# The last expert's rows by one-hot products, and the first token-MLP products taken pass by pass

## The reference, cut to what matters

```python
x = x + attention(conditioned(x))
x = x + routed_ffn(expert_ffn(x))        # 2nd: routed_ffn is the part below
x = x + mingru(token_mlp(x))             # 3rd: token_mlp, two picked experts of width 1024 and a shared one
x = x + ffn(adapted(x))

def routed_ffn(h):                       # 8 experts, top 2, room for 640 tokens each
    ...
    exp_batches = zeros(8, 640, 256).at[flat_e, pos_safe].set(x[tok], mode='drop')
    h = gelu(inp) * gate                 # inp, gate = split(exp_batches @ W1), width 512
    exp_out = h @ W2                     # [8, 640, 256]
    gathered = exp_out[flat_e, min(pos_safe, 639)]
    contrib = where(keep, gates_f, 0)[:, None] * gathered
    return segment_sum(contrib, tok)     # each token: two gated rows of exp_out
```

## Time and profile before

| | |
|---|---|
| time, median of 3 runs | 999.74 us (998.01 to 1001.44) |
| profiled execution, own time | 1008.6 us |
| span of the profile | 1007.4 us |
| PE busy | 953.5 us, 95% of the span |
| DVE / ACT / POOL busy | 497.4 / 436.1 / 272.2 us |
| DMA | 67.48 MB moved, mean 67 GB/s |
| DMA queue of SP (q1) / of POOL (q0) | 11.2% / 9.3% of 16 engines |

### The profile page before, as it was taken

How to read it: one execution, slowest core, us unless ns; L and a number is a source line. 1 busy time by engine, 2 the same in 40 slices (tenths; PEclk the granted TensorE clock), 3 DMA queues, 4 the chain that set the end, 5 groups by cost and what they waited for, 6 DMA issues and landing times.

```text
span 1007.4 us, 13258 instructions
## 1 busy us (share of the span) xinstructions
PE 953.5 (95%) x4952; PEld 783.0 (78%) x4952; DVE 497.4 (49%) x947; ACT 436.1 (43%) x820; POOL 272.2 (27%) x243
## 2 busy tenths in 40 slices
PE   5989999999899999999699999999999999998998
PEld 2667767787589999987587788888888888876786
DVE  5645453566444554544467433333333333688544
ACT  2555564523154444544234334244343342326675
POOL 1333221402256555536452014023041140100000
PEclk9999999999999999999999999999999999999999
DMA  7130001102325444441521300302003003000011
GB/s 261 43 106 21 22 1 64 73 22 84 122 47 125 133 114 133 115 152 35 190 57 39 126 1 1 126 0 110 16 1 126 1 0 126 1 1 1 1 42 43
DMA packets 21648, 67.48 MB, mean 67 GB/s; under 512 B 4497, under 2 KB 11921, under 8 KB 19281
## 3 DMA queue, kind: packets, MB, share of 16 engines
q1 hardware_dynamic: 16592, 39.88, 11.2%
q0 software_dynamic: 4704, 26.49, 9.3%
q10 hardware_dynamic: 288, 0.26, 0.1%
HBM read 55.09 MB, written 9.44 MB: 64 GB/s over the span
## 4 chain that ended last, share of the span: by engine, by line
PE 72%; DVE 12%; ACT 6%; issue 4%; DMA 3%; another core or an unknown queue 1%; SPq 1%; DVEq 0%; ACTq 0%; POOLq 0%
PE banks L934 15%; PE banks L936 14%; PE banks L935 14%; PE banks L1132 4%; PE banks L1133 4%; PE banks L1131 4%; PE banks L1014 3%; PE banks L998 2%; PE banks L1181 1%; PE banks L1180 1%; PE banks L1167 1%; PE banks L1168 1%; PE banks L950 1%; PE banks L1005 1%; DMA expert_output<-y_rows 1%
## 5 line engine op out<-in xcount | busy, mean ns | idle before, releaser
L934 PE MATMUL banks<-input_hi,mlp_hi 128*128 128x512 f32 (+1 forms) x396 | 156.1, 394 | 3.9 <-DVE input_lo L1741 2.4
L936 PE MATMUL banks<-input_hi,mlp_lo 128*128 128x512 f32 (+1 forms) x396 | 155.3, 392 | 0.0
L935 PE MATMUL banks<-input_lo,mlp_hi 128*128 128x512 f32 (+1 forms) x396 | 154.8, 391 | 0.0
L1937 POOL TENSOR_TENSOR mlp_lo<-weight_stage,mlp_hi 128x768 fp32r<-128x768 f32 x40 | 73.6, 1841 | 241.8 <-ACT mlp_hi L1369 241.8
L1384 ACT CAST hidden_hi<-hidden 128x512 fp32r<-128x512 f32 x96 | 59.6, 621 | 176.4 <-DVE hidden L1751 108.0
L1757 DVE TENSOR_TENSOR hidden_lo<-hidden,hidden_hi 128x512 fp32r<-128x512 f32 x96 | 66.5, 693 | 71.3 <-ACT hidden_hi L1384 71.3
L1751 DVE SCALAR_TENSOR_TENSOR hidden<-banks,L_expert_weight,gelu 128x512 f32<-128x512 f32 x64 | 48.0, 751 | 97.6 <-PE banks L936 97.4
L1907 POOL TENSOR_TENSOR ffn_w_lo<-weight_stage,ffn_w_hi 128x512 fp32r<-128x512 f32 x48 | 62.0, 1294 | 109.2 <-ACT ffn_w_hi L1331 109.2
L934 PEld LDWEIGHTS banks<-input_hi,mlp_hi 128*128 128x128 f32 x396 | 75.2, 190 | 20.2 <-issue 4.3
L936 PEld LDWEIGHTS banks<-input_hi,mlp_lo 128*128 128x128 f32 x396 | 75.3, 190 | 16.4
L935 PEld LDWEIGHTS banks<-input_lo,mlp_hi 128*128 128x128 f32 x396 | 75.5, 191 | 16.0
(11 more groups left out here) (298 smaller groups left out, 2099.2 us busy)
## 6 DMA issues: line engine op xcount, KB each, us to landing
weight_stage<-in_packF SPq DMA_DIRECT2D x8, 1536.0 KB, 6.9
weight_stage<-in_shared SPq DMA_DIRECT2D x2, 3072.0 KB, 10.9
expert_output<-y_rows SPq DMA_DIRECT2D x40, 128.0 KB
weight_stage<-in_cond_w SPq DMA_DIRECT2D x4, 512.0 KB, 6.4
...
```

The costliest lines, as they stand in the source:

```text
L934: pe.matmul(o, wh, dh, start=(i == 0), stop=False)
L935: pe.matmul(o, wh, dl, start=False, stop=False)
L936: last = pe.matmul(o, wl, dh, start=False, stop=(i == len(terms) - 1))
L1937: pool.tensor_tensor(wDl[s][:, qs], stage[:, qs], f(wDh[s][:, qs]), ALU.subtract).then_inc(done)
```

## The change

1. *Chunk 0 without the last expert's rows in DRAM.* For chunk 0 the contribution of expert 7 no longer goes through the table. For each of its five slot tiles DVE makes a one-hot matrix `hot` (is slot s of token t, 128x512), beside expert 6's down products. After each `w2` of expert 7, ACT makes the gated rounded row tile (`hot_hi`) and DVE the difference (`hot_lo`); after the last `w2` PE multiplies them by `hot` into banks 0 and 1 (`hot`, 20 products of 512 columns), DVE adds the two banks to `xT` (`hot_add`), ACT and DVE make the halves (`hot_in`, `hot_in_lo`).
2. *Chunk 0's other seven experts are combined beside expert 7* (`beside_last_expert`): `fetch`, `comb`, `yt` and `add` of tiles 0 to 3 are woven into it; the fetch waits for the stores of experts 0 to 6. For chunk 0 the row numbers and the gates of expert 7 are set to zero.
3. *The gate of each slot of expert 7* comes by a table in DRAM: SP writes 2048 gates, one element a descriptor, after the routing; POOL reads them by five indirect DMAs and numbers 512 columns (`counting`), at the start of expert 2. Both gate and token rows are shifted by one, so that row 0 is an unused slot's.
4. *The first MLP weights earlier and in halves.* `ld_mlp` becomes two loads of 1.5 MB, for all phases. Half 0 goes out once expert 6's weights are split, half 1 once expert 7's are. Pieces 0 to 4 are split beside expert 6's down products, pieces 5 to 7 in the first three steps of expert 7.
5. *First products pass by pass.* The early halves are gone; the first two units wait for `hot_in` of each block and use `inL` last (`first_products`).
6. *Fillers.* `slots` 8 to 16, `first rows` 27 to 13; the 30 and 7 ahead of the first tiles go, 4 come ahead of the first MLP product.
7. The combining of chunks 1 to 3 starts one unit later.

```diff
-EARLY = 3
+HOT = 0
...
-SPIN = {"first scores": 12, "logits": 5, "slots": 8, "first rows": 27, "first tile": 30, "next tile": 7}
+SPIN = {"first scores": 12, "logits": 5, "slots": 16, "first rows": 13, "first hidden": 4}
...
-        if e + 1 == G:
-            pool.append(("ld_mlp", 0))
+        if e + 2 >= G:
+            pool.append(("ld_mlp", 0, e + 2 - G))
...
+            if e == G - 1:
+                act.append(("hot_hi", j))
+                dve.append(("hot_lo", j))
             dve.append(("yrow", e, j))
+            if e == G - 2:
+                dve.append(("onehot", j))
+                mlp_piece(j)
...
+    def mlp_piece(q):
+        act.append(("wm_hi", 0, q))
+        pool.append(("wm_lo", 0, q))
+    def beside_last_expert():
+        for tt in range(3):
+            pool.append(("fetch", tt))
+        for q in range(ST, PIECES):
+            mlp_piece(q)
+            if q == ST:
+                pool.append(("fetch", 3))
+            yield
+        yield
+        for tt in range(2):
+            dve.append(("comb", tt))
+            yield
+        for tt in range(3):
+            product("turn3", "yt", tt)
+            if tt == 0:
+                dve.append(("comb", 2))
+            dve.append(("add", tt))
+            yield
+        dve.append(("comb", 3))
+        yield
+        yield
+        product("turn3", "yt", 3)
+        dve.append(("add", 3))
...
-            run(weave(expert, split_mlp(0)))
...
+            run(weave(expert, beside_last_expert()))
...
+    banks["hot", 0] = (HOT, HOT + 1)
+    assert ring_at["work"] % 4 == HOT
+    ring_at["work"] += KD
+    for j in range(ST):
+        pe.append(("hot", j))
+    for k in range(KD):
+        dve.append(("hot_add", k))
+        act.append(("hot_in", k))
+    for k in range(KD):
+        dve.append(("hot_in_lo", k))
+    spin(SPIN["first hidden"], HOT + KD)
...
-        if tt < 2:
-            spin(SPIN["next tile"] if tt else SPIN["first tile"], 4)
-        product("first_yt" if tt < QT else "work", "yt", tt)
+        product("work", "yt", tt)
...
-    use("first_yt", [(4,), (5,)])
-    for n, _ in enumerate(combine_tiles(0, QT)):
-        if n >= QT // 2 + 1:
-            early_half(n - QT // 2 - 1)
-    pool.append(("ld_mlp", 1))
+    for half in range(2):
+        pool.append(("ld_mlp", 1, half))
...
-                pool.append(("ld_mlp", n + 2))
-            next(combining, None)
+                for half in range(2):
+                    pool.append(("ld_mlp", n + 2, half))
+            if n or u:
+                next(combining, None)
...
+        def first_products(o, terms, s):
+            for k, (wh, wl, dh, dl) in enumerate(terms):
+                pe.wait_ge(*ready("hot_in", k))
+                pe.matmul(o, wh, dh, start=(k == 0), stop=False)
+                pe.matmul(o, wl, dh, start=False, stop=False)
+            for k, (wh, wl, dh, dl) in enumerate(terms):
+                pe.wait_ge(*ready("hot_in_lo", k))
+                last = pe.matmul(o, wh, dl, start=False, stop=(k == KD - 1))
+            last.then_inc(s)
...
+            elif kind == "hot":
+                j, = key
+                if j == 0:
+                    for i in range(ST):
+                        pe.wait_ge(*ready("onehot", i))
+                pe.wait_ge(*ready("hot_lo", j))
+                for k in range(KD):
+                    ks = slice(k * P, (k + 1) * P)
+                    pe.matmul(banks[:, HOT + k, :], y7H[:, j, ks], hot[:, j, :], start=(j == 0), stop=False)
+                    last = pe.matmul(banks[:, HOT + k, :], y7L[:, j, ks], hot[:, j, :], start=False, stop=(j == ST - 1))
+                last.then_inc(done)
...
+                if n == 0 and u < 2:
+                    first_products(o, [(wh[:, k, ms], wl[:, k, ms], inH[:, k, sl(0)], inL[:, k, sl(0)]) for k in range(KD)], done)
...
-                    pe.wait_ge(*ready("xe_lo", G - 1, ST - 1))
-                    pe.wait_ge(*ready("yrow", G - 1, ST - 1))
+                    pe.wait_ge(*(ready("yrow", G - 1, ST - 1) if c else ready("add", QT - 1)))
...
+                act.wait_ge(ld[name if name == "mlp" else name + str(q // (PIECES // 2))], 16 * turn)
                 if n == 0:
-                    act.wait_ge(*ready("w1", G - 2, 1, IT - 1, 1))
-                    act.wait_ge(*ready("w2", G - 2, ST - 1))
+                    act.wait_ge(*(ready("w1", G - 2, 1, IT - 1, 1) if (q + 1) * PIECE <= 4 * KD * I0 else ready("w2", G - 2, ST - 1)))
...
+                act.activation(y7H[:, j, :], bank(("w2", G - 1, j))[:, 0:D], ACT.Copy, scale=slot_gate[:, j:j + 1]).then_inc(done)
...
+                act.copy(inH[:, k, sl(0)], xT[:, k, sl(0)]).then_inc(done)
...
+                dve.tensor_scalar(hot[:, j, :], counting[:, :], slot_number[:, j:j + 1], None, ALU.is_equal).then_inc(done)
...
+                dve.scalar_tensor_tensor(y7L[:, j, :], bank(("w2", G - 1, j))[:, 0:D], slot_gate[:, j:j + 1], f(y7H[:, j, :]), ALU.mult, ALU.subtract).then_inc(done)
...
+                dve.wait_ge(*ready("hot", ST - 1))
+                dve.tensor_tensor(xT[:, k, sl(0)], banks[:, HOT + k, :], xT[:, k, sl(0)], ALU.add).then_inc(done)
...
+            elif kind == "gate_of_slot":
+                pool.iota(counting[:, :], [[1, CH]], base=1, channel_multiplier=0, allow_small_or_imprecise_dtypes=True).then_inc(ramps)
+                pool.wait_ge(ld["gate_table"], 16)
+                for j in range(ST):
+                    n = (G - 1) * ST + j
+                    pool.indirect_dma_start(slot_gate[:, j:j + 1], None, gate_rows, bass.IndirectOffsetOnAxis(ap=slot_token[:, n:n + 1], axis=0)).then_inc(ld["gate_of_slot"], 16)
...
+                pool.indirect_dma_start(stage[:, half * PK1 // 2:(half + 1) * PK1 // 2], None, A[f"pack1_{half}"], bass.IndirectOffsetOnAxis(ap=dyn1[:, m:m + 1], axis=0)).then_inc(ld[f"picked_mlp{half}"], 16)
...
+                        pool.wait_ge(st_y[i], 16 * len(range(i, (G - 1) * ST, 4)))
+                    pool.wait_ge(*ready("back_gates"))
+                    pool.wait_ge(*ready("xe", G - 1, ST - 1))
+                elif tt == QT:
...
+        sp.wait_ge(*ready("back_gates"))
+        sp.dma_start(gate_rows[1:1 + N, :].rearrange("(n p) a -> p (n a)", p=P), last_gate, allow_slow_non_contiguous=True).then_inc(ld["gate_table"], 16)
```

154 lines of the change are left out of this document (100 added, 54 removed).

## The result

The changed kernel takes 1011.49 us (median of 5 runs, 1007.74 to 1012.76) against 999.74 us before (median of 5, 998.01 to 1001.44). The ratio is 1.0111, with an interval of 1.0092 to 1.0131; a second session gave 1.0088 (1.0057 to 1.012). The forecast was 979 us, so it was wrong in sign. In both sessions the kernel before took 1000 us. Where it takes 1008, there are only single runs of both (1012.88 against 1007.89 and 1010.06 us), 0.3 to 0.5% apart.

The account below looks back on a forecast made before the run. The prediction took PE, busy 95% of the span, as the bound. Its terms, -4.4 - 14.4 - 2.7 + 0.7 = -20.8 us, scaled to 20.7 off 999.7, gave 979 us, with an 8 in 10 range of 973 to 990.

Parts of the forecast that it names:

- a: Expert 7: 23.15 us in place of 27.53, -4.4 us, with the new DVE and POOL work nearly hidden.
- The part on the store: Expert 7: the 10.17 us store takes 5 beside half the load, leaving nothing or a few tenths of the stop.
- 7.2 us in 22 us, of which DVE uses about half: Expert 7: new DVE work of four `comb`, four `add` and five `hot_lo` was set against DVE's half-used time.
- The one-hots: Expert 6's down steps: 0.486 us each on DVE, hidden; at three times that, up to 0.7 us a step shows.
- b: Expert 7's last down product to the MLP's third unit: 14.7 us in place of 29.16, -14.4 us.
- c: First expert: with the third gather landing at 276.4, the first product starts at 277.95, not 280.66; -2.7 us.
- R3: Gate table's 2048 small packets delay expert 0's gathers, 0.042 to 0.162 us a packet; dear end 1005 us; chance 0.05.
- The threshold of 0.20 us a packet: Gate table: packet price from which the small-packet delay decides, (20.8 + 5.2) x 16 / 2048, only without queues taking turns.
- d: Combining of chunks 1 to 3 one unit later: one more unit has both a piece and a tile, +0.7 us.
- e: Work taken as free: gate gathers and numbering (7.5 us of POOL, 9.9 free, expert 2), small DVE operations, half loads.
- R1: Second weights' load beside expert 7 delays its row store, last copy and `hot_add`; +6.2, 985 us; chance 0.13.
- R2: Expert 7: DVE stops at `comb` until the fetch is there, three tiles 1.5 us late; +4.5, 983.5 us; chance 0.16.

Follow-up runs that it names:

- e4: Changed kernel with POOL's fetch of tile 3 moved behind the sixth to eighth pieces of the MLP's split; 1014.2 us, ratio 1.0046 to before.
- e5: Changed kernel, unchanged, timed again beside the kernel before and traced; 1009.42 against 999.89 us, ratio 1.0088.
- e6: Changed kernel without the gate table and its gathers; DVE multiplies the one-hot banks by a row of 512 gates; 998.59 us, 0.9999 of before.
- e2: Changed kernel with the gate table written as 128 rows of 64 bytes, not 2048 elements of 4; 1007.4 against 1008.5 us before, ratio 0.9977.
- e12: Changed kernel with 50 fillers of 512 columns on PE between the second and third tile's transposes; a single run of 1012.97 us.
- e16: Changed kernel, unchanged, traced beside the kernel before on one chip; a single run of 1012.88 us.
- e9: e6 with pieces ahead of fetches, each one-hot between `hidden` and `expert_hidden_lo` of expert 7's steps four to eight, combs in its down stage; 0.9906 of before.
- e13: e9 with the second MLP weights' load in the MLP's third unit, not beside expert 7's down products; 992.55 against 1004.94 us, 0.9871 of before.

## Why the prediction was wrong

**a, expert 7 (forecast 23.15, measured 31.97).** The part on the store came true: in the first trace no copy of expert 7's stretch waited for a store, but the last, 0.39 us. The failed sentence is "7.2 us in 22 us, of which DVE uses about half". It was read from busy time. In a step DVE is bound to 1.51 of 1.80 us, and 7.2 us of new work didn't fit: with a comb behind it a step took 2.41 us (`hidden` at 468.60 and 471.01). In addition POOL's pieces stop `expert_hidden_lo` for as long as they run. The row that said so was there in the trace of before, unread: seven times in expert 7 that operation took 0.81 to 0.86 us beside a piece, and 0.49 elsewhere. POOL's order made it worse: the sixth piece stood behind six fetches (458.35 to 465.7), the last two behind the fetch of tile 3, which waited for `yt` of tile 0 (468.83), so they ran in a row at 471.93, and PE stood 3.97 us. A smaller term put at nothing is "only three of its eight steps carry a piece": ACT's loop makes each of them 0.34 us longer than PE needs, 1.0 us in all. Behind that stop the products ran at the lower clock, 1.2 GHz (PEclk, the third number from the end):

```profile
477.00:481.00 4.00, 3.94 (x19) 3.95 (x20) 2.42 (x8) 1.31 (x3) 0.94 (x1) 0.50 0.85 301
```

So the down stage took 14.3 us, where expert 5's takes 7.9, and the up stage 17.65 in place of 14.4.

The Trainium skill ("SBUF — State Buffer", Who interferes with whom) says that a DVE instruction with two SBUF inputs contends with a GpSimd instruction that reads SBUF, and calls the shared port pair an exclusive lock. The traces agree, 5.11 us beside 5.37 in e4, and add that POOL's next operations, if they stand ready, go first.

**The one-hots (forecast 0.486 each, hidden).** Measured 1.39 to 1.96. I had kept "three times that" as the dear end and took the alone price although the pieces stood beside them by plan. Expert 6 grew from 22.35 to 24.8 us, which had no term at all in the sum.

**b, to the third unit (forecast 14.7, measured 14.85).** Right, with its parts: one-hot products 4.57 us (485.73 to 490.30), then 1.68 to the first MLP product, 8.6 for three units. The saving is 12.7 to 14.3 us, by which of the traces of before it is counted against.

**c, the first expert (forecast -2.7, measured +8.0 from first trace to first trace, +6.5 between the medians of five and of three).** The gain itself is real: counted from the third gather's start, the first product comes 1.6 to 3.3 us sooner in the versions without small packets. (The sum as written, 276.4 + 1.41, gives 277.81 and not 277.95, a slip of 0.14 us.) The step that failed is R3's dismissal, "I take the cheap end, since these are SP's packets like the stores", and its "only if the queues don't take turns". R3's mechanism was the right one, given 0.05, but not its picture of gathers that stand behind the whole table: the third gather was issued before the table (273.33 and 273.86) and landed at 286.92, while the table took until 291. Both queues' packets passed, and POOL's were slow. The price was (17.2 x 16 / 2048) 0.134 us a packet, near the dear end of 0.162, not the 0.042 of the stores. The threshold of 0.20 us a packet was right only against a gain of 20.8; part c came out 10.7 worse than forecast, expert 7 8.8 and expert 6 2.4.

**d, combining one unit later (forecast +0.7, measured +0.9).** The units with a piece and a tile last 5.0 to 5.1 us, as read; five of them before and six now (not eight), and the added one took 4.2. That the stretch from the first `dn` to the end is as long as before (506.1 and 506.2 us) is luck: the first unit behind that `dn` became 0.8 us shorter (4.97 and 4.17), which the forecast had not.

**e, "no cost".** The gathers of gates cost 2.5 us in expert 2 from e5 to e6, and 5.8 to 6.6 in two other sessions (30.0 and 30.1 in e2, e4 and e12 against 23.4 to 24.2 in the traces without them). The failed step is "where POOL has 22.5 - 12.59 = 9.9 us free": that is its time in the whole expert, and not where its next work waits. In e5 and in the first trace the five issues held back two splits of weights, which then ran in a row and kept `expert_hidden_lo` for 3.55 us, theory L again. In e2, e4 and e12 that operation stayed at 0.49 us there; what makes 6 us of it is open (see the end). The small DVE operations and the halves of later loads showed no cost.

**The sum.** First trace to first trace: c +8.0, expert 0 +1.4, experts 1 to 5 -2.6, expert 6 +2.4, expert 7 +4.4, b -14.3, in all -0.7, as the spans say. The timed runs say +9 to +12. These traces show no more than a guess at the difference, the 5.2 us of experts 1 to 5 told above; the rest is open. R1 was no part of it in the changed kernel (its last copy waited for a store 0.39 us in the first trace, 1.04 in e5 and 2.68 in e16, and "to dn" was 14.85 or 14.84 in all three), but the difference of e9 and e13, some 3 us, is its kind, once the earlier stops are gone. R2 had the right stretch, at half of what it cost, by another mechanism: it has DVE stop at `comb` until the fetch is there, and none of the four combs of expert 7 waited for its fetch in the changed kernel's first trace.
